# A pre-norm attention and expert layer on one core: where the attended values are transposed and divided

## The chip, the cores and the metric

One core of one Trainium2 chip. The metric is the device time of one execution, in microseconds (us). The kernel is written engine by engine: TensorE (PE) multiplies, VectorE (DVE), ScalarE (ACT) and GpSimd (POOL) work on elements, and SyncE (SP) issues every DMA. Each engine takes its instructions in program order, and they are tied together by semaphores.

## What is computed

The input is x, 32 sequences of 256 tokens of 128 features. Two residual layers follow each other. The first is attention with 16 heads of 8 features and a window of 128 tokens, the second a mixture of 16 experts of width 64 (4 chosen for each token, from 2 of 4 groups) beside one shared expert.

```python
x = x + attention(layernorm(x))        # softmax over keys j with i-128 <= j <= i, then @ w_out.T + b_out
x = x + experts(layernorm(x))          # sigmoid router, top 4 of 16, silu(g) * u, shared expert
def attention(x):
    q, k, v = split(x @ w_in.T + b_in)               # 16 heads of 8
    scores = where(allowed, q @ k.T / sqrt(8), -1e9)
    return (softmax(scores) @ v) @ w_out.T + b_out
```

All inputs and outputs are float32.

## The kernel before

The 8192 tokens are worked in 16 steps of 512 tokens (two sequences, called halves 0 and 1 below). All 16 steps of attention come first, then all 16 steps of experts; the rows after attention (x1) wait in device memory between the two.

**Attention.** The function `body(i)` of each engine holds one period of a software pipeline: the scores, exponentials and attended values of step i-1 ("now") and the projections and row maxima of step i ("prep"). Before the exponentials of a step the kernel needs the maximum of each row of scores. So TensorE first computes the scores once for their maxima (`score_maxima`, units 0 to 7 of a step, four per half; each unit fills two banks of PSUM, `ps_max`), VectorE reduces each bank to chunk maxima (`chunk_maxima`, line 910, two instructions per unit), and after four units `row_maxima` (lines 929 to 939) makes the row maxima, which SyncE writes to memory and loads back into the operands of the second computation (`load_max`). A unit may start only when both banks of the unit before it are reduced, since there is one pair of banks. The second computation is `scores` (units 0 to 9, five per half), whose two banks ScalarE turns into probabilities (`exps`, line 699); unit u+1 of `scores` waits for the exponentials of unit u, since there is again one pair of banks. `attend` and `attend_tails` multiply the probabilities with the values; the values carry a column of ones, so the sum of each row comes out beside them, in `ps_att`, transposed: features on partitions, tokens along the row.

**From attended values to x1, before.** ScalarE copies `ps_att` to SBUF (`take_att`, line 708); TensorE transposes it into `ps_b` (`transpose_att`, line 1434, four transposes per half); VectorE takes the reciprocal of the row sums and multiplies (`normalise`, lines 947 and 950); TensorE transposes the quotient into `ps_c` (`transpose_attn`, line 1448, two per half); ScalarE copies that (`take_attn`, line 716); TensorE multiplies with the output weights (`project_att`, line 1458); and VectorE adds the residual (`add_residual`, line 962).

**What else a period holds.** VectorE makes the statistics of the layer norm of the next step (`statistics(prep + 1)`, lines 867 and 874), spreads the queries (`spread_q`, line 888, four instructions) and makes the low parts of queries and keys (`low_part`, line 898). GpSimd normalises the next step (lines 521 to 536) and adds a constant vector to x for the residual (`residual`, line 552). When that sum is done, SyncE loads the next x into the same buffer (`load_x`, line 412), and `statistics` waits for that load. TensorE projects queries, keys (`project_qk`, line 1284) and values (`project_v`, line 1291) and transposes the normalised x (`transpose_x`, line 1270). ScalarE spreads the values (`spread_v`, line 687).

**What sets the order.** Nothing is scheduled by a tool: the order on each engine is that of the calls in its `body`, `last` (the last attention step, which also prepares the expert weights) and the loop over `d` for the experts.

**Experts.** Each step d has nine rounds. In each, TensorE computes gate and up projections of two experts (`up`, lines 1603 to 1605), ScalarE applies silu (line 799), VectorE multiplies (`gate`, line 1140), GpSimd multiplies by the routing weights (`weigh`, line 634), and TensorE multiplies down (`down`, line 1614). The routing of step d+2 is computed between the rounds. The 16 weights of each token are made by GpSimd (`scale_weight`, line 624), transposed by TensorE (`transpose_weights`, line 1591), copied by ScalarE (line 791), stored to memory and loaded back broadcast over 64 partitions (`store_weight`, `load_spread`).

The order of TensorE in a period of attention:

```python
scores(now, 5); attend(now, 0, 1); score_maxima(prep, 2); attend_tails(now, 0)
scores(now, 6); transpose_att(now, 0); score_maxima(prep, 3)
scores(now, 7); transpose_attn(now, 0); attend(now, 1, 0)
scores(now, 8); score_maxima(prep, 4); transpose_x(prep + 1); project_att(now, 0)
scores(now, 9); score_maxima(prep, 5); attend(now, 1, 1); attend_tails(now, 1); score_maxima(prep, 6)
```

## Time and profile before

| | us |
|---|---|
| median of 3 runs | 753.68 (753.0 to 758.73) |
| the profiled execution | 755.73 |
| its span, first to last instruction | 754.0 |
| TensorE busy in the span | 707.3 (94%) |
| VectorE busy | 580.1 (77%) |
| ScalarE busy | 364.2 (48%) |
| GpSimd busy | 299.5 (40%) |

The profile is one execution. Its rows give for each instruction the engine, the line of the kernel, the operation, output and input tiles, the start from the span's beginning and the duration. In a timeline several instructions of a line stand merged in one row, and the duration is then that of all; the ends of matmuls are modelled and overlap the next row, so what a piece of TensorE's work occupies is read from one start to the next. The attention steps fill the span from about 16 to 390 us, the experts from 394 us to the end.

### The profile page before, as it was taken

To read this page: it belongs to the slowest core of one execution; us is meant where nothing else is said; L and a number is where in the kernel's file an instruction comes from. 1 tells how busy PE (TensorE), PEld (TensorE's weight loads), DVE (VectorE), ACT (ScalarE), POOL (GpSimd) and SP (SyncE) were. 2 spreads that over 40 slices of the span, in tenths; PEclk is the share of its full clock that TensorE was granted. 3 is DMA by queue.
4 is the path that set the end of the run, shared out by engine and by line. 5 is a ranking of instruction groups with operands and counts; after the bars stand their busy time and mean duration, and the time that the engine had idled before them with its cause. 6 is when DMAs were issued, how large, how long until landed. Compare 5 with 4: busy or idle time off the path is not lost.

```text
span 754.0 us, 21748 instructions
## 1 busy us (share of the span) xinstructions
PE 707.3 (94%) x8499; PEld 472.1 (63%) x8499; DVE 580.1 (77%) x1745; ACT 364.2 (48%) x740; POOL 299.5 (40%) x320
## 2 busy tenths in 40 slices
PE   5697999899999999999778999999999999999997
PEld 3364666666666666666455666666666666666664
DVE  6676878788888888888477878887877888777632
ACT  3365666667677667666562332332333233233321
POOL 5212112122221122212205665666656666664543
PEclk9599999999999999999889999999999999999999
DMA  2244222233323232333118356664445666544560
GB/s 85 61 135 129 63 96 67 83 102 103 101 80 100 84 90 67 95 102 102 59 48 206 76 126 154 155 151 103 120 122 130 154 156 142 112 105 106 118 140 28
DMA packets 64885, 80.23 MB, mean 106 GB/s; under 512 B 10976, under 2 KB 38896, under 8 KB 64752
## 3 DMA queue, kind: packets, MB, share of 16 engines
q1 hardware_dynamic: 64784, 78.84, 40.0%
q8 instruction: 68, 1.11, 0.6%
q14 instruction: 33, 0.27, 0.1%
HBM read 61.00 MB, written 17.56 MB: 104 GB/s over the span
## 4 chain that ended last, share of the span: by engine, by line
PE 78%; DVE 8%; DMA 6%; ACT 4%; issue 2%; SPq 2%; POOL 1%; DVEq 0%; ACTq 0%; PEldq 0%; POOLq 0%
PE ps_c L1614 14%; PE ps_att L1399 7%; PE ps_sc L1373 6%; PE ps_max L1603 4%; PE ps_max L1329 4%; PE ps_max L1605 4%; PE ps_max L1604 4%; PE ps_sc L1347 4%; PE ps_sc L1604 4%; PE ps_sc L1605 4%; PE ps_sc L1603 4%; PE ps_a L1291 3%; ACT probs L699 3%; DMA xin<-in_L_attn_x_dram 2%; DVE chunkmax L910 2%; PE ps_c L1617 2%
## 5 line engine op out<-in xcount | busy, mean ns | idle before, releaser
L634 POOL TENSOR_TENSOR probs<-probs,stacks 128x512 f32<-128x512 f32 x128 | 165.1, 1290 | 125.8 <-DVE probs L1140 74.1
L799 ACT ACTIVATE probs<-ps_max 128x512 f32<-128x512 f32 x144 | 86.1, 598 | 220.2 <-PE ps_max L1605 216.6
L910 DVE TENSOR_REDUCE chunkmax<-ps_max 128x14 f32<-128x448 f32 (+1 forms) x250 | 151.7, 648 | 36.4 <-PE ps_max L1306 36.3
L699 ACT ACTIVATE probs<-ps_sc 128x512 f32<-128x512 f32 x256 | 138.9, 595 | 50.6 <-PE ps_sc L1347 49.6
L1140 DVE TENSOR_TENSOR probs<-probs,ps_sc 128x512 f32<-128x512 f32 x128 | 87.2, 682 | 69.5 <-PE ps_sc L1605 26.3
L1614 PE MATMUL ps_c<-probs,wd 128*128 128x512 f32 x256 | 130.3, 592 | 1.3 <-POOL probs L634 1.3
L1603 PE MATMUL ps_max<-xh,whigh 128*128 128x512 f32 x144 | 93.4, 649 | 2.9 <-DVE probs L1140 2.1
L552 POOL TENSOR_TENSOR xres<-xin,cvec 128x512 f32<-128x512 f32 x16 | 20.5, 1282 | 141.5 <-DVE x L962 141.1
L1373 PE MATMUL ps_sc<-stacks 32*64 32x192 f16 (+2 forms) x2048 | 64.4, 232 | 11.4 <-ACT probs L699 2.6
L1399 PE MATMUL ps_att<-probs,stacks 128*32 128x192 f32 (+1 forms) x1536 | 71.0, 319 | 0.0
L1373 PEld LDWEIGHTS ps_sc<-stacks 32*64 32x64 f16 x2048 | 36.6, 105 | 44.1 <-ACT probs L699 26.5
L521 POOL TENSOR_TENSOR veps<-meanvar,eps 128x4 f32<-128x4 f32 x32 | 6.4, 201 | 140.8 <-DVE meanvar L874 140.8
L1604 PE MATMUL ps_max<-xl,whigh 128*128 128x512 f32 x144 | 57.0, 396 | 0.0
L1605 PE MATMUL ps_max<-xh,wlow 128*128 128x512 f32 x144 | 56.9, 395 | 0.0
L1614 PEld LDWEIGHTS ps_c<-probs,wd 128*128 128x128 f32 x256 | 48.2, 189 | 13.5 <-POOL probs L634 1.7
L1329 PE MATMUL ps_max<-hl,qdiag 32*128 32x160 f16 x1000 | 48.6, 216 | 8.0 <-DVE chunkmax L910 7.1
L1399 PEld LDWEIGHTS ps_att<-probs,stacks 128*32 128x32 f32 x1536 | 44.2, 112 | 16.8 <-issue 3.1
L1604 PE MATMUL ps_sc<-xl,whigh 128*128 128x512 f32 x128 | 50.8, 397 | 0.0
L1605 PE MATMUL ps_sc<-xh,wlow 128*128 128x512 f32 x128 | 50.8, 397 | 0.0
L1603 PE MATMUL ps_sc<-xh,whigh 128*128 128x512 f32 x128 | 50.5, 394 | 0.0
L1347 PE MATMUL ps_sc<-edges,repeat 64*128 64x192 bf16 (+2 forms) x576 | 49.9, 243 | 0.0
L1329 PEld LDWEIGHTS ps_max<-hl,qdiag 32*128 32x128 f16 x1000 | 31.2, 93 | 26.6 <-DVE chunkmax L910 15.0
(167 smaller groups left out, 1253.7 us busy)
## 6 DMA issues: line engine op xcount, KB each, us to landing
stacks<-weight_scratch SPq DMA_DIRECT2D x32, 1024.0 KB, 9.9
stacks<-qk_scratch SPq DMA_DIRECT2D x48, 256.0 KB, 3.2
qk_scratch<-hl SPq DMA_DIRECT2D x32, 256.0 KB, 3.5
xin<-in_L_attn_x_dram SPq DMA_DIRECT2D x16, 256.0 KB, 3.5
x_scratch<-x SPq DMA_DIRECT2D x16, 256.0 KB, 2.2
xin<-x_scratch SPq DMA_DIRECT2D x16, 256.0 KB, 9.1
xres<-x_scratch SPq DMA_DIRECT2D x16, 256.0 KB, 9.3
out_dram<-result SPq DMA_DIRECT2D x16, 256.0 KB, 9.2
```

What stands on the lines that cost most here:

```text
L634: nc.gpsimd.tensor_tensor(inter[p % 3], gated[p % 2], spread[d % 2][:, p, :], ALU.mult).then_inc(inter_ready, 1)
L699: nc.scalar.activation(dst[:, :], ps_sc[s][:, 0:dst.shape[1]], ACT.Exp, scale=SCALE).then_inc(probs_ready, 1)
L799: nc.scalar.activation(silu[n % 2][rows, :], ps_max[n % 2][rows, :], ACT.Silu).then_inc(silu_ready, 1)
L910: nc.vector.tensor_reduce(chunkmax[:, 2 * pair + m, at:at + CHUNKS[h]], max_banks(d, u)[m][:, 0:BANK_COLS[h]].rearrange("p (n k) -> p n k" ...
L1140: tt(gated[p % 2], silu[n % 2], ps_sc[n % 2][:, :], ALU.mult).then_inc(gated_ready, 1)
L1329: mm(banks[m][:, at:at + width], qdiag[rows, b * NB + n, :, :].rearrange("p c k -> p (c k)"), hl[rows, 0, 1, b * S + key0:b * S + key0 + w ...
L1373: mm(dst, qkstack[p][rows, 1, jj, q0:q0 + TB], qkstack[p][rows, 0, jj, q0:q0 + QCOLS[m]].rearrange("p (n k) -> p n k", k=TB), start=(at == ...
L1399: last = mm(ps_att[32 * x:32 * x + 32, half * S + TB * m:half * S + TB * m + QCOLS[m]].rearrange("p (n k) -> p n k", k=TB), vdiag[p][:, (b ...
L1603: mm(bank[slot][:, :], whigh[:, q, :], xh[d % 3][:, :], start=True, stop=False)
L1604: mm(bank[slot][:, :], whigh[:, q, :], xl[d % 3][:, :], start=False, stop=False)
L1605: last = mm(bank[slot][:, :], wlow[:, q, :], xh[d % 3][:, :], start=False, stop=True)
L1614: last = mm(ps_c[:, :], wd[:, p, :], inter[p % 3], start=(p == 0), stop=False)
```

## The change

**Attended values.** ScalarE's two copies and TensorE's six transposes per half are gone. VectorE transposes `ps_att` by blocks of 32x32 into `att_rows` (`take_att`, one instruction of 128x512), divides there (`normalise`, which writes the features in another order), and transposes the quotient again by blocks of 32x32 into `attTn` (128x256). The output weights are put into the same order once at the start, for which ScalarE makes one copy more and TensorE one transpose more, and one more copy and transpose serve the constant vector.

**Chunk maxima.** The two banks of a unit are one tensor now, reduced by one instruction.

**Orders.** TensorE's order in `body` is another (below), and ScalarE spreads the values after unit 6 of the exponentials instead of after unit 4. GpSimd's `residual` also waits for `spread_q` of its step.

**Routing weights.** VectorE transposes them by blocks of 32x32 (`transpose_weights`, 128x64, after round 1 of a step), SyncE stores them with four DMAs instead of one, and TensorE's four transposes and ScalarE's copy per step are gone.

```diff
@@ SyncE, store_weight
-                sp.wait_ge(weightT_ready, d + 1)
+                sp.wait_ge(weightQ_ready, d + 1)
                 after(sp, spread_loaded[d % 2], 32 * (d // 2))
-                sp.dma_start(wt_d[d % 2], weightT[d % 2][:, :]).then_inc(weight_stored[d % 2], 16)
+                dst = wt_d[d % 2].rearrange("n t -> (n t)").rearrange("(b q i k) -> i q b k", b=2, q=32, i=4, k=32)
+                for i in range(4):
+                    sp.dma_start(dst[i], weightQ[d % 2][32 * i:32 * i + 32, :].rearrange("q (b k) -> q b k", b=2)
+                                 ).then_inc(weight_stored[d % 2], 16)
@@ GpSimd, residual
                 after(pool, x1_ready, 2 * d - 2)
+                pool.wait_ge(qdiag_ready, d + 1)
                 pool.wait_ge(x_loaded[d % 2], 16 * (d // 2 + 1))
@@ ScalarE, body
                 exps(now, 4)
+                exps(now, 5)
+                exps(now, 6)
...
                 spread_v(prep)
-                exps(now, 5)
-                take_att(now, 0)
-                exps(now, 6)
                 exps(now, 7)
-                take_attn(now, 0)
@@ VectorE
-                for m in range(2):
-                    dve.wait_ge(max_full, 16 * d + 2 * u + m + 1)
-                    nc.vector.tensor_reduce(chunkmax[:, 2 * pair + m, at:at + CHUNKS[h]],
...
+                dve.wait_ge(max_full, 8 * d + u + 1)
+                nc.vector.tensor_reduce(chunkmax[:, 2 * pair:2 * pair + 2, at:at + CHUNKS[h]],
+                                        max_banks(d, u)[:, :, 0:BANK_COLS[h]].rearrange("p m (n k) -> p m n k", k=KB),
+                                        AX.X, ALU.max).then_inc(max_free, 1)
...
+            def take_att(d, b):
...
+                dve.wait_ge(pv_done, 6 * d + 3 * b + 3)
+                after(dve, att_ready, 2 * d + b)
+                nc.vector.transpose(att_rows[:, :], ps_att[:, :]).then_inc(att_rows_ready, 1)
...
-                view = ps_b[:, :].rearrange("p (n k) -> p n k", k=16)
-                dve.wait_ge(att_tr_done, 2 * d + b + 1)
+                view = att_rows[:, :].rearrange("p (n k) -> p n k", k=16)
+                dve.wait_ge(att_rows_ready, 2 * d + b + 1)
                 nc.vector.reciprocal(rden[:, :], view[:, :, HD]).then_inc(nd_chain, 1)
                 dve.wait_ge(nd_chain, 2 * d + b + 1)
...
+                nc.vector.tensor_tensor(att[:, :].rearrange("p (n h d) -> p h n d", h=2, d=HD),
+                                        att_rows[:, :].rearrange("p (h n k) -> p h n k", h=2, k=16)[:, :, :, 0:HD],
+                                        rden[:, :].rearrange("p (h n) -> p h n", h=2).unsqueeze(3).to_broadcast([P, 2, 16, HD]),
+                                        ALU.mult).then_inc(att_ready, 1)
+                dve.wait_ge(att_ready, 2 * d + b + 1)
+                after(dve, proj_done, 2 * d + b)
+                nc.vector.transpose(attTn[:, :], att[:, :]).then_inc(attTn_ready, 1)
@@ VectorE, body
                 chunk_maxima(prep, 2)
+                take_att(now, 0)
                 normalise(now, 0)
...
                 add_residual(now, 0)
+                take_att(now, 1)
                 chunk_maxima(prep, 6)
...
@@ TensorE, body
                 scores(now, 0)
-                transpose_att(now - 1, 1)
                 project_v(prep, 0)
                 score_maxima(now, 7)
+                project_v(prep, 3)
                 scores(now, 1)
-                transpose_attn(now - 1, 1)
...
                 score_maxima(prep, 2)
+                scores(now, 6)
                 attend_tails(now, 0)
-                scores(now, 6)
-                transpose_att(now, 0)
+                project_v(prep, 2)
                 score_maxima(prep, 3)
                 scores(now, 7)
-                transpose_attn(now, 0)
                 attend(now, 1, 0)
+                score_maxima(prep, 4)
                 scores(now, 8)
-                score_maxima(prep, 4)
                 transpose_x(prep + 1)
```

TensorE, from the attended values of half 1 (`attend(now, 1, 0)`) to the transposes of x, before. `ps_sc` with `stacks` are the scores (unit 8), `ps_max` with `hl` the maxima (unit 4):

```order
L1399 MATMUL ps_att<-probs,stacks 32x192 x8
L1399 MATMUL ps_att<-probs,stacks 32x128 x4
L1373 MATMUL ps_sc<-stacks 64x3x64 x8
L1373 MATMUL ps_sc<-stacks 64x2x64 x4
L1347 MATMUL ps_sc<-edges,repeat 128x192 x2
L1347 MATMUL ps_sc<-edges,repeat 128x128 x2
L1329 MATMUL ps_max<-hl,qdiag 128x160 x6
L1329 MATMUL ps_max<-hl,qdiag 128x32 x2
L1306 MATMUL ps_max<-edges,repeat 128x3x2x32 x2
L1306 MATMUL ps_max<-edges,repeat 128x32 x2
L1270 MATMUL ps_a<-ident,xhat 128x128 x4
```

The same place in the changed program (line numbers are its own):

```order
L1396 MATMUL ps_att<-probs,stacks 32x192 x8
L1396 MATMUL ps_att<-probs,stacks 32x128 x4
L1327 MATMUL ps_max<-hl,qdiag 128x160 x6
L1327 MATMUL ps_max<-hl,qdiag 128x32 x2
L1304 MATMUL ps_max<-edges,repeat 128x3x2x32 x2
L1304 MATMUL ps_max<-edges,repeat 128x32 x2
L1370 MATMUL ps_sc<-stacks 64x3x64 x8
L1370 MATMUL ps_sc<-stacks 64x2x64 x4
L1344 MATMUL ps_sc<-edges,repeat 128x192 x2
L1344 MATMUL ps_sc<-edges,repeat 128x128 x2
L1268 MATMUL ps_a<-ident,xhat 128x128 x4
```

The maxima of unit 4, which wait for VectorE's reduction of unit 3, stood behind the scores of unit 8 and now stand ahead of them.

VectorE, from the statistics to the row maxima, before:

```order
L867 BN_STATS stats<-xin 128x6 x4
L874 BN_AGGR meanvar<-stats 128x2 x4
L910 TENSOR_REDUCE chunkmax<-ps_max 128x16 x2
L947 RECIPROCAL rden<-ps_b 128x32
L950 TENSOR_TENSOR att<-ps_b,rden 128x256
L910 TENSOR_REDUCE chunkmax<-ps_max 128x14 x2
L929 TENSOR_REDUCE rowmax<-chunkmax 128x4x3
```

The same place in the changed program:

```order
L839 BN_STATS stats<-xin 128x6 x4
L846 BN_AGGR meanvar<-stats 128x2 x4
L881 TENSOR_REDUCE chunkmax<-ps_max 128x2x16
L918 STREAM_TRANSPOSE att_rows<-ps_att 128x512
L926 RECIPROCAL rden<-att_rows 128x32
L929 TENSOR_TENSOR att<-att_rows,rden 128x2x16x8
L935 STREAM_TRANSPOSE attTn<-att 128x256
L881 TENSOR_REDUCE chunkmax<-ps_max 128x2x14
L900 TENSOR_REDUCE rowmax<-chunkmax 128x4x3
```

Between the chunk maxima of units 2 and 3 two instructions (lines 947 and 950) have become four, and each pair of reductions is one of twice the columns.

## Rows read from the trace of the kernel before

**Rows 1.** Busy us by stretch: PE, PEld, DVE, ACT, POOL; then clock, DMA share, GB/s.
```profile
200.00:300.00 100.00, 97.91 (x2074) 65.88 (x2072) 85.42 (x249) 69.26 (x146) 22.82 (x25) 1.00 0.27 86
...
500.00:600.00 100.00, 100.00 (x403) 66.85 (x401) 82.86 (x261) 32.47 (x62) 61.28 (x58) 1.00 0.59 140
```

**Rows 2.** Timeline, TensorE (start us, us, line, tiles).
```profile
201.37 0.66 PE L1434 MATMUL ps_b<-ident,attT 128*128 128x128 f32 x4
201.96 0.37 PE L1329 MATMUL ps_max<-hl,qdiag 32*128 32x160 f16 x8
...
202.49 0.41 PE L1373 MATMUL ps_sc<-stacks 32*64 32x192 f16 x12
...
203.08 0.44 PE L1448 MATMUL ps_c<-ident,att 128*128 128x128 f32 x2
203.45 1.08 PE L1399 MATMUL ps_att<-probs,stacks 128*32 128x192 f32 x24
204.45 0.41 PE L1373 MATMUL ps_sc<-stacks 32*64 32x192 f16 x12
...
206.51 0.32 PE L1373 MATMUL ps_sc<-stacks 32*64 32x64 f16 x16
...
208.68 0.40 PE L1329 MATMUL ps_max<-hl,qdiag 32*128 32x160 f16 x8
...
222.74 0.66 PE L1434 MATMUL ps_b<-ident,attT 128*128 128x128 f32 x4
```

**Rows 3.** Timeline, VectorE, same stretch.
```profile
203.97 0.58 DVE L929 TENSOR_REDUCE rowmax<-chunkmax 128x12 f32<-128x60 f32 x6
...
204.80 0.21 DVE L939 STREAM_TRANSPOSE rowmaxT<-rowmax 128x32 f16<-128x32 f16 x1
...
214.04 2.07 DVE L888 TENSOR_SCALAR qdiag<-hl,headrow 128x512 f16<-128x512 f16 x4 [0.24 <-ACT hl L672]
...
220.27 0.86 DVE L867 BATCH_NORM_STATS2 stats<-xin 128x6 f32<-128x128 f32 x4
...
221.60 1.26 DVE L910 TENSOR_REDUCE chunkmax<-ps_max 128x16 f32<-128x512 f32 x2
```

**Rows 4.** Timeline, GpSimd: the residual sum and the centring.
```profile
201.99 1.04 POOL L526 TENSOR_TENSOR xcent<-xin,meanvar 128x512 f32<-128x512 f32 x1
...
213.88 1.29 POOL L552 TENSOR_TENSOR xres<-xin,cvec 128x512 f32<-128x512 f32 x1 [9.72 <-DVE x L962]
```

**Rows 5.** Line 888, VectorE, whole span (ns min/median/max).
```profile
L888 DVE TENSOR_SCALAR qdiag<-hl,headrow x64: 334/341/1282, 14.4 to 342.5; 128x512 f16<-128x512 f16 x64
```

**Rows 6.** VectorE groups by form, 100 to 340 us.
```profile
L910 DVE TENSOR_REDUCE chunkmax<-ps_max 128x16 f32<-128x512 f32 x90 | 57.4, 679 | 9.5 <-PE ps_max L1306 9.5
L910 DVE TENSOR_REDUCE chunkmax<-ps_max 128x14 f32<-128x448 f32 x92 | 52.9, 616 | 13.8 <-PE ps_max L1306 13.8
...
L950 DVE TENSOR_TENSOR att<-ps_b,rden 128x256 f32<-128x256 f32 x23 | 9.8, 424 | 0.8
...
L947 DVE RECIPROCAL rden<-ps_b 128x32 f32<-128x32 f32 x23 | 8.1, 352 | 4.3 <-PE ps_b L1434 4.3
...
L939 DVE STREAM_TRANSPOSE rowmaxT<-rowmax 128x32 f16<-128x32 f16 x23 | 4.9, 211 | 0.8
```

**Rows 7.** Line 412, the loads of x, 100 to 340 us.
```profile
DMA to landing us min/median/max: 3.0/3.6/4.5
```

**Rows 8.** VectorE groups by form, 430 to 700 us.
```profile
L1122 DVE TENSOR_TENSOR chosen<-picked,score 128x64 f32<-128x64 f32 x12 | 15.2, 1269 | 0.4
...
L1119 DVE TENSOR_TENSOR picked<-replaced,ps_a 128x64 f32<-128x64 f32 x12 | 2.6, 213 | 0.0
```

**Rows 9.** Timeline, TensorE, experts.
```profile
581.26 0.60 PE L1591 MATMUL ps_b<-ident,weight 128*16 128x128 f32 x4
581.62 0.48 PE L1603 MATMUL ps_max<-xh,whigh 128*128 128x512 f32 x1
```

**Rows 10.** Timeline, GpSimd, between the two phases.
```profile
403.02 1.26 POOL L634 TENSOR_TENSOR probs<-probs,stacks 128x512 f32<-128x512 f32 x1 [5.37 <-DMA stacks<-weight_scratch]
```

More of the change, by code:

```diff
@@ L170, in build_block @@
         share = sb("share", [P, NT], FP32)
[L171 to L172 removed]
+        weight = sb("weight", [P, NE, NT], FP32)
+        weightQ = [sb(f"weightQ{p}", [P, NE * NT], FP32) for p in range(2)]
         silu = [probs[n][:, :] for n in (0, 1)]
@@ L1132, in shares, with transpose_weights @@
                 nc.vector.reciprocal(share[:, :], total1[:, :]).then_inc(share_ready, 1)
+            def transpose_weights(d):
+                if not valid(d):
+                    return
+                dve.wait_ge(weight_ready, d + 1)
+                after(dve, weight_stored[d % 2], 64 * (d // 2))
+                nc.vector.transpose(weightQ[d % 2][:, :], weight[:, :, :].rearrange("p n t -> p (n t)")
+                                    ).then_inc(weightQ_ready, 1)
             def gate(d, p):
@@ L1176, in last @@
                 split_weight(3)
+                take_att(now, 0)
                 normalise(now, 0)
@@ L1193, in last @@
                 invert(1)
+                take_att(now, 1)
                 normalise(now, 1)
@@ L1338, in score_maxima @@
                         g = 2 * pair + m
-                        last = masks(banks, m, [window], slice(32 * g, 32 * g + 32), (32 * g, 0))
-                        if w == len(windows) - 1:
-                            last.then_inc(max_full, 1)
+                        last = masks([banks[:, n, :] for n in range(2)], m, [window], slice(32 * g, 32 * g + 32), (32 * g, 0))
+                last.then_inc(max_full, 1)
             def mask2(s, cols, edge):
@@ L1463, in _ @@
             pe.wait_ge(w_loaded, 16 * 2)
-            for n in range(4):
-                last = nc.tensor.transpose(ps_b[:, n * P:(n + 1) * P], wraw[:, n, :], ident[:, :])
-            last.then_inc(wt_done, 1)
+            for n in range(3):
+                nc.tensor.transpose(ps_b[:, n * P:(n + 1) * P], wraw[:, n, :], ident[:, :])
+            pe.wait_ge(wo_turned, 1)
+            nc.tensor.transpose(ps_b[:, 3 * P:4 * P], wo_order[:, :], ident[:, :]).then_inc(wt_done, 1)
+            nc.tensor.transpose(ps_sc[0][:, 0:E], wraw[:, 3, :], ident[:, :]).then_inc(wo_done, 1)
             pe.wait_ge(b_loaded, 16 * 2)
@@ L1530, in transpose_weight @@
                         last = nc.tensor.transpose(bank[:, t * P:(t + 1) * P], xhat[:, t, :], ident[:, :])
-                elif what[0] == "weight":
-                    pe.wait_ge(weight_ready, 1)
-                    for t in range(NT):
-                        last = nc.tensor.transpose(bank[0:NE, t * P:(t + 1) * P], weight[:, t, :], ident[:, :])
-                    last.then_inc(weight_tr_done, 1)
-                    pe.wait_ge(weight_tr_done, 1)
-                    pe.sem_inc(fw_done, 1)
-                    return
                 elif what[0] == "sh":
@@ L1582, in route @@
                 last.then_inc(logit_done, 1)
-            def transpose_weights(d):
-                if not valid(d):
-                    return
-                pe.wait_ge(weight_ready, d + 1)
-                after(pe, result_ready, d - 2)
-                for t in range(NT):
-                    last = nc.tensor.transpose(ps_b[0:NE, t * P:(t + 1) * P], weight[:, t, :], ident[:, :])
-                last.then_inc(weight_tr_done, 1)
             def up(d, p):
```

159 lines of the change are left out of this document (50 added, 109 removed).

## The prediction

> **What bounds the kernel now.** I read the busy time by stretch first. In attention TensorE is busy in 97.9 of 100 us at the full clock and VectorE in 85.4; among the experts TensorE is busy in all of 100 us and VectorE in 82.9 [rows 1]. So TensorE sets the pace of both phases, but in attention VectorE stands only 15% behind it. Then the timeline of TensorE. The same transpose of half 0 comes at 201.37 and at 222.74 [rows 2], so a period of attention lasts 21.37 us, and there are 15 of them between the first body and the last step. In that timeline scores follow scores: unit 7 starts at 202.49 and unit 8 at 204.45 [rows 2]. Unit 8 needs the exponentials of unit 7, and 1.96 us is what that round through ScalarE costs; whatever TensorE does inside it is free. From unit 9 at 206.51 to the maxima of unit 6 at 208.68 [rows 2] lie 2.17 us of work in one piece. The timeline of VectorE then shows what its part of a period is made of [rows 3, 6].
>
> **What leaves TensorE.** Per half, four transposes from 201.37 to 201.96 and two from 203.08 to 203.45 [rows 2]: 0.59 + 0.37 = 0.96 us, so 1.9 us per period. If TensorE stayed the bound, a period would be 21.37 - 1.9 = 19.5 us; since some of these transposes lie inside a 1.96 us round, 20.0 is nearer. That is the first rival. ScalarE loses copies that nobody is short of.
>
> **What VectorE gains and loses.** (a) The first transposition, 128x512 float32 out of PSUM. The trace has only one such operation, 128x32 in float16, at 211 ns [rows 6]. For the slope I use the reductions: 679 against 616 ns for 64 columns more [rows 6], 0.98 ns a column. 211 + 480 x 0.98 = 0.68 us, and the reduction of 512 columns says the same. I take 0.7. Below, it will hardly beat that reduction, so 0.68; above, float32 may cost two passes, 211 + 2 x 480 x 0.98 = 1.15 us. (b) The second, 128x256 in SBUF: 211 + 224 x 0.98 = 0.43 us, with 0.42 (the product of that shape [rows 6]) and 0.65 as ends. (c) Two reductions of 679 become one of 679 + 512 x 0.98 = 1.18, and two of 616 one of 616 + 448 x 0.98 = 1.06. Before, such a pair took 1.26 us [rows 3], since the second starts before the first is quite done, so a unit wins 0.08 at most, 0.6 per period. (d) The four spreading instructions take 2.07 us together [rows 3], though the median of one is 0.34 and the longest 1.28 [rows 5]: the first of them waits out GpSimd's residual sum, which runs from 213.88 to 215.17 [rows 4]. With the new wait GpSimd comes after them, and 0.94 us per period is won. (e) The multiplication (0.42 [rows 6]) read PSUM and SBUF and now reads SBUF twice. Among the experts the product of two SBUF tiles takes 1.27 us while its neighbour of the same shape with one operand in PSUM takes 0.21 [rows 8]; it waits out a GpSimd instruction. In attention GpSimd's centring of 1.04 us [rows 4] and what follows it lie just behind the statistics, where the division of half 0 now comes.
>
> In sum VectorE has per period 2 x (0.7 + 0.43) = 2.3 us more and 1.5 less. It was busy for 0.854 x 21.37 = 18.3 us and will be for about 19.1. That is too near 20 to be hidden by itself, so the order of waits decides.
>
> The Trainium skill (SBUF — State Buffer, Who interferes with whom) says that a VectorE instruction with two SBUF inputs and a GpSimd instruction that reads SBUF fully block each other, the later one waiting for the earlier. Rows 8 agree. By that rule (e) costs between nothing and one GpSimd instruction at half 0; the sum below carries 0.3 for it, from the rows.
>
> The Trainium skill (Vector Engine (DVE) Microarchitecture Reference, The reshape front-end and per-opcode configuration) says that a transposing instruction sustains one element per cycle and lane, and makes no exception for four-byte elements. No row here shows a float32 one. By that rule the two-pass price of (a) falls away; I keep it as a rival, since only a run can tell.
>
> **The loop that closes.** In the new order each thing waits for the one before, all around a period. I start where `attend_tails` of half 1 is done.
> 1. VectorE: transposition 0.75 with its hand-over; maxima 6, 1.13; division of half 1 (reciprocal 0.36, product 0.42, transposition 0.43, links) 1.23; maxima 7, 1.00; row maxima 1.04, from 203.97 to 204.80 + 0.21 [rows 3]; residual add, of the product's shape, 0.35; spreading 2.07 - 0.94 = 1.13. Together 6.6.
> 2. Only now GpSimd: residual sum 1.29 [rows 4]; only then SyncE loads the next x, which lands after 3.6 us (3.0 to 4.5) [rows 7]; hand-overs 0.2. Together 5.1. Beside it the low parts and maxima 0 and 1 of VectorE are done in about 4.5, so VectorE waits some 0.6 for x.
> 3. VectorE: statistics from 220.27 to 221.60, 1.33 [rows 3]; maxima 2, 1.13; transposition 0.75; division of half 0, 1.23, with 0.3 for GpSimd. Together 4.7.
> 4. Maxima 3, 1.06 and 0.06 to TensorE. TensorE: maxima 4, 0.5 (as from 201.96 to 202.49 [rows 2]), which now stand ahead of scores 8; the round from scores 8 to scores 9, 1.96; from scores 9 to the end of the tails 2.17 and 0.1. Together 5.9.
>
> Sum 22.3 us. Before, the loop was open at step 4 (scores 8 stood ahead of maxima 4, so a late reduction of unit 3 did not delay them) and in step 2 (GpSimd started beside the spreading). I take 22.1 for the period, 0.7 over the old one: the landing is as often below as above 3.6, and not each link will be the last in each period. TensorE, 1.9 us lighter, then waits some 2.5 us in each period for VectorE. Over 15 periods: +10.5 us (21.5 to 22.8: +2 to +21).
>
> **The rest.** Among the experts four transposes go from 581.26 to 581.62 [rows 9], 0.36 us, with the change of kind around them up to 0.6, in 15 steps: -6 us (-5 to -9). VectorE does 128x64 instead, 0.25 us, behind round 1, where it has 15% of idle time; four stores instead of one take SyncE some 1 us more, but start earlier. Between the phases GpSimd waits 5.4 us for the first weights at 403.02 [rows 10]; they leave TensorE's queue, where they stood behind eight other transposes, so -1 (-2 to +1). The start has two copies and two transposes more: +0.5 (0 to 1).
>
> Sum: 10.5 - 6 - 1 + 0.5 = +4. The profiled execution took 755.73 us, so its like would take 759.7; the median of the runs shown is 753.68, 2 us lower, and the forecast against it is 757.7, with a range of its own of 750 to 768.
>
> **Rivals.** What differs by 1%, 7.5 us, can be told from no change.
> - TensorE stays the bound: the load of x lands early, the reductions keep ahead, and a period is 20.0 us. 15 x 1.4 = 21 and 6 and 1 less: 726 us. For it speaks VectorE's busy sum of 19.1, below 20; against it, that steps 1 to 4 are serial by the semaphores and VectorE would have no idle time at all, though it now waits for TensorE before most reductions [rows 6]. Chance 0.13. Between it and the forecast (21.4 or less, 747 or under) another 0.05.
> - The forecast: 0.62. About a quarter of it lies above 1%.
> - Two passes for float32: 0.45 us more for each first and 0.22 for each second transposition, all four in the loop: 22.1 + 1.3 = 23.4, so 757.7 + 15 x 1.3 = 777 us. It decides from about 0.9 us per 128x512. Against it, the float16 row pays hardly anything over other small operations. Chance 0.08.
> - The product of half 0, and the spreading, run into GpSimd again: where maxima 2 come 0.3 later than I put them, the product finds not the end of the centring but the whole next instruction, 1.04 instead of 0.3, and GpSimd's output comes later to TensorE too. 15 x 0.8 = 12: 770 us. Chance 0.12.
>
> Faster by over 1% then has 0.13 + 0.05 = 0.18, slower 0.08 + 0.12 + 0.16 = 0.36, and 0.46 lies within. The range leaves out the first rival and the dearest: 746 to 773.
>
> **What would show it.** Right: a period of 21.8 to 22.4 between two equal rows of TensorE; TensorE waiting about 1.2 us for line 881 before the maxima of unit 4 in each period, and below 92% busy from 100 to 340 us; the statistics of VectorE waiting for the load of x in most periods, which they do in hardly any now; spreading instructions all near 0.34; the 128x512 transposition at 0.7. Wrong: VectorE idle before its reductions as before with TensorE still at 98%, which would be the first rival; a transposition of over 0.9 us; products of over 1 us in the division. Among the experts TensorE stays at 100% and a step is 0.4 us shorter.

## The result, and the profile after

| | before | after |
|---|---|---|
| median of the runs | 755.51 us (753.0 to 758.73) | 765.67 us (763.82 to 770.84) |
| the profiled execution | 755.73 | 770.84 |
| its span | 754.0 | 769.0 |
| mean granted clock of TensorE in it | 0.974 | 0.946 |
| TensorE, VectorE, ScalarE busy | 707.3, 580.1, 364.2 | 693.9, 593.0, 330.0 |

The changed kernel takes 1.0143 times the time of before (95% interval 1.0074 to 1.0213), some 10 us more. The profiled execution, 770.84, is the longest of its four runs; a second profile of the same kernel (below) has a span of 762.4 us at a clock of 0.959. Runs more than 1.5% above the fastest of the same kernel are left out of all medians and ratios.

The busy time by stretch, after (columns as in [rows 1]; 100:200 is new beside them):

```profile
100.00:200.00 100.00, 89.22 (x1893) 58.83 (x1892) 82.70 (x214) 57.63 (x119) 19.69 (x21) 0.96 0.25 78
200.00:300.00 100.00, 85.34 (x1912) 56.80 (x1912) 81.14 (x207) 57.33 (x120) 22.05 (x25) 0.98 0.29 92
...
500.00:600.00 100.00, 100.00 (x392) 66.50 (x391) 82.22 (x262) 31.54 (x62) 62.64 (x61) 1.00 0.54 128
```

TensorE fell from 97.9 to 85.3 us of 100 in attention and is still at 100 among the experts. VectorE has more work in all, but not a greater share of each 100 us (81 to 83 against 85.4): neither engine is full, so what grew is waiting. The clock column matters later: before it is 1.00 from 100 to 300 us, and here it is 0.96 and 0.98.

One piece of VectorE's and of TensorE's timeline, after. This is the stretch that steps 3 and 4 of the forecast describe:

```profile
205.66 0.87 DVE L839 BATCH_NORM_STATS2 stats<-xin 128x6 f32<-128x128 f32 x4 [1.71 <-DMA xin<-in_L_attn_x_dram]
...
207.00 1.19 DVE L881 TENSOR_REDUCE chunkmax<-ps_max 128x32 f32<-128x1024 f32 x1
208.11 0.71 DVE L918 STREAM_TRANSPOSE att_rows<-ps_att 128x512 f32<-128x512 f32 x1
...
209.24 0.52 DVE L929 TENSOR_TENSOR att<-att_rows,rden 128x256 f32<-128x256 f32 x1
209.79 0.45 DVE L935 STREAM_TRANSPOSE attTn<-att 128x256 f32<-128x256 f32 x1
210.16 1.05 DVE L881 TENSOR_REDUCE chunkmax<-ps_max 128x28 f32<-128x896 f32 x1
```

```profile
208.25 0.37 PE L1327 MATMUL ps_max<-hl,qdiag 32*128 32x160 f16 x8 [1.47 <-DVE chunkmax L881]
...
208.65 0.41 PE L1370 MATMUL ps_sc<-stacks 32*64 32x192 f16 x12
...
211.27 0.40 PE L1327 MATMUL ps_max<-hl,qdiag 32*128 32x160 f16 x8 [0.96 <-DVE chunkmax L881]
...
211.70 0.41 PE L1370 MATMUL ps_sc<-stacks 32*64 32x192 f16 x12
```

The statistics wait 1.71 us for the load of x. Everything behind them is late by it: the reduction of unit 2 releases TensorE's maxima 3 at 208.25 after 1.47 us of idle time, the reduction of unit 3, behind the four instructions of the division, releases maxima 4 at 211.27 after 0.96. Scores 7 (208.65) and scores 8 (211.70) are 3.05 us apart, where [rows 2] had 1.96. In a period of after in which no load is late they are still 2.86 apart (230.36 and 233.22).

The waits between 100 and 340 us, eleven periods (us in total, times, longest):

```profile
DVE chunkmax L881 <- PE ps_max L1304: 22.2, 28, 2.9
...
PE ps_max L1327 <- DVE chunkmax L881: 16.0, 20, 1.7
...
DVE stats L839 <- DMA xin<-in_L_attn_x_dram: 4.6, 3, 1.9
```

Before, over the same stretch:

```profile
PE ps_max L1329 <- DVE chunkmax L910: 0.2, 1, 0.2
```

VectorE waited for TensorE's maxima before too (23.3 us, 46 times). What is new is the other direction, 16.0 us in which TensorE waits for the reductions. And one period on the chain of waits of after:

```profile
267.87 1.14 POOL xres L557
269.01 5.36 DMA xin<-in_L_attn_x_dram
...
278.98 0.99 DVE chunkmax L881
...
280.01 0.40 PE ps_max L1327 x8
```

In this period the chain passes through the steps of the forecast one by one, with a load of x that took 5.4 us where I had 3.6. The row above it misleads, as an experiment showed: GpSimd's residual sum is not what held this load back.

**Where the 15 us of the two profiled executions lie.** The first and the last of the spreadings of the queries mark 15 periods, TensorE's first gate projection marks the experts. After:

```profile
L860 DVE TENSOR_SCALAR qdiag<-hl,headrow x64: 342/348/355, 14.4 to 359.3; 128x512 f16<-128x512 f16 x64
```

```profile
L1555 PE MATMUL ps_max<-xh,whigh x144: 395/794/798, 414.0 to 759.4; 128*128 128x512 f32 x144
```

The same row of before for the projections ([rows 5] has the spreadings, 14.4 to 342.5):

```profile
L1603 PE MATMUL ps_max<-xh,whigh x144: 466/762/798, 394.2 to 744.4; 128*128 128x512 f32 x144
```

| us | start | 15 periods | between the phases | experts | at 1.2 GHz, 30 to 350 us |
|---|---|---|---|---|---|
| before | 14.4 | 328.1 | 51.7 | 359.8 | 13 |
| after | 14.4 | 344.9 | 54.7 | 355.0 | 40 |
| after, again | 14.9 | 337.6 | 53.6 | 356.3 | 22 |

The last column is summed from the granted clock in stretches of 4 us: a stretch at 0.57 is mostly at 1.2 GHz, one at 1.00 wholly at 2.4 GHz. Up to 350 us, all of it lies ahead of 100 us in before; in after 16 us lie behind. Between the phases every kernel here has some: from 352 to 464 us before has 14 us and after 30.

### The profile page after: what moved, and what is told of

It reads as the page before. It is cut to its first block, busy times and chain, and to the rows that moved or that the text cites. A ratio compares the mean times of both kernels' runs of the same rounds, so it can differ in the third digit from the quotient of the medians.

```text
span 769.0 us, 21082 instructions
## 1 busy us (share of the span) xinstructions
PE 693.9 (90%) x8244; PEld 458.8 (60%) x8244; DVE 593.0 (77%) x1697; ACT 330.0 (43%) x662; POOL 301.5 (39%) x320
## 4 chain that ended last, share of the span: by engine, by line
PE 64%; DVE 18%; issue 6%; DMA 6%; ACT 3%; SPq 1%; POOL 1%; DVEq 0%; ACTq 0%
PE ps_c L1566 14%; DVE chunkmax L881 5%; PE ps_max L1555 5%; PE ps_max L1557 4%; PE ps_max L1556 4%; PE ps_att L1396 4%; DMA xin<-in_L_attn_x_dram 4%; PE ps_sc L1370 4%; PE ps_sc L1556 4%; PE ps_sc L1555 4%; PE ps_sc L1557 4%; PE ps_max L1327 3%; PE ps_sc L1344 3%; DVE att_rows L918 2%; PE ps_c L1569 2%
## 5 line engine op out<-in xcount | busy, mean ns | idle before, releaser
L881 DVE TENSOR_REDUCE chunkmax<-ps_max 128x28 f32<-128x896 f32 (+1 forms) x125 | 142.2, 1138 | 35.6 <-PE ps_max L1304 35.3
L1370 PE MATMUL ps_sc<-stacks 32*64 32x192 f16 (+2 forms) x2048 | 67.0, 240 | 17.1 <-ACT tails L704 6.9
L1327 PE MATMUL ps_max<-hl,qdiag 32*128 32x160 f16 x1000 | 50.2, 221 | 34.2 <-DVE chunkmax L881 27.7
L1396 PE MATMUL ps_att<-probs,stacks 128*32 128x192 f32 (+1 forms) x1536 | 76.1, 336 | 0.0
L1370 PEld LDWEIGHTS ps_sc<-stacks 32*64 32x64 f16 x2048 | 38.2, 109 | 50.2 <-issue 20.9
L1396 PEld LDWEIGHTS ps_att<-probs,stacks 128*32 128x32 f32 x1536 | 46.1, 116 | 18.2 <-issue 0.7
L1555 PEld LDWEIGHTS ps_max<-xh,whigh 128*128 128x128 f32 x144 | 27.5, 191 | 39.1 <-issue 37.0
```

What stands on the lines that cost most here:

```text
L881: nc.vector.tensor_reduce(chunkmax[:, 2 * pair:2 * pair + 2, at:at + CHUNKS[h]], max_banks(d, u)[:, :, 0:BANK_COLS[h]].rearrange("p m (n k ...
L1327: mm(banks[:, m, at:at + width], qdiag[rows, b * NB + n, :, :].rearrange("p c k -> p (c k)"), hl[rows, 0, 1, b * S + key0:b * S + key0 + w ...
L1370: mm(dst, qkstack[p][rows, 1, jj, q0:q0 + TB], qkstack[p][rows, 0, jj, q0:q0 + QCOLS[m]].rearrange("p (n k) -> p n k", k=TB), start=(at == ...
L1396: last = mm(ps_att[32 * x:32 * x + 32, half * S + TB * m:half * S + TB * m + QCOLS[m]].rearrange("p (n k) -> p n k", k=TB), vdiag[p][:, (b ...
L1555: mm(bank[slot][:, :], whigh[:, q, :], xh[d % 3][:, :], start=True, stop=False)
```

## The experiments

Ratios are to the kernel before, run beside each group of experiments (medians 755.55 us for the first four, 756.58 for the next four, 755.72 for the last four), with 95% intervals. They are not made from the two medians, and times of different groups are compared only to 1 us or so.

**The changed kernel once more,** unedited, as the ground for the next ones.

> The changed kernel once more, as the one to compare the others of this call with. Expected as measured: 1.010 to 1.018 of the kernel before, TensorE waiting 1.0 us or more for line 881 ahead of the maxima of unit 4, and the statistics waiting for the load of x in some periods.

Measured: 762.80 us, 1.0100 (1.0064 to 1.0136). Together with the first result the loss is 1.0 to 1.4%. In what follows after is 762.8.

**The load of x first.** SyncE takes its work in order too, and in its body the next x stood behind the loading back of the row maxima and the store of x1.

```diff
@@ SyncE, body
+                load_x(i + 1)
                 load_max(i - 1, 1)
                 store_x1(i - 2)
-                load_x(i + 1)
```

> Only SyncE's order changes: load_x of a period is issued ahead of the second load_max and the store of x1, which it does not depend on. Theory A (the landing of x, issued behind the round trip of the row maxima, is in the loop that closes a period): the statistics wait for no load, a period is about 0.4 us shorter and the long ones of over 23 us are gone, 6 to 10 us less than the changed kernel. Rival B (the loop is closed by VectorE and TensorE alone, the load is beside it): no change, within 2 us.

Measured: 753.22 us, 0.9976 (0.995 to 1.0002): 9.6 us less than after, from this one move. The queue of SyncE and GpSimd's residual sum, after:

```profile
221.04 0.33 SPq L400 DMA_DIRECT2D max_scratch<-rowmaxT  x1
...
222.46 0.55 SPq L402 DMA_DIRECT2D stacks<-max_scratch  x1
222.47 1.27 POOL L557 TENSOR_TENSOR xres<-xin,cvec 128x512 f32<-128x512 f32 x1 [11.81 <-issue]
...
223.54 0.43 SPq L413 DMA_DIRECT2D xin<-in_L_attn_x_dram  x1
```

and with the load first:

```profile
207.71 0.44 SPq L413 DMA_DIRECT2D xin<-in_L_attn_x_dram  x1
...
215.80 1.26 POOL L557 TENSOR_TENSOR xres<-xin,cvec 128x512 f32<-128x512 f32 x1 [11.82 <-issue]
...
220.33 0.86 DVE L839 BATCH_NORM_STATS2 stats<-xin 128x6 f32<-128x128 f32 x4
```

In after the load starts at 223.54, while this period's residual sum still runs (until 223.74): it doesn't wait for that sum but for the one before, long done, and was held only by its place behind the store (221.04) and the loading back (222.46) of the row maxima and the store of x1. Moved ahead it starts 8 us before the residual sum, and the statistics wait for nothing. Its 15 periods are 334.1 us (337.6 without) and the stretch between the phases 49.6 (53.6): the same queue also carries the x1 that the experts' first statistics need. So of the 9 us between these two executions 3.5 lie in the periods and 4.0 between the phases. The forecast for the period itself was missed: its commonest length stays 21.52 us, and three periods of over 23 us are left (26.5, 23.4 and 24.6), all three with a clock below 1.00. The late load is not what makes the period long where the clock is full.

**Maxima 4 behind scores 8,** as before, alone and with the load first.

```diff
@@ TensorE, body
                 attend(now, 1, 0)
-                score_maxima(prep, 4)
                 scores(now, 8)
+                score_maxima(prep, 4)
```

> Only TensorE's order changes: the maxima of unit 4 stand behind the scores of unit 8 again, as before the change. Theory A: the late reduction of unit 3 no longer holds up scores 8, and a period is 0.65 us shorter, 10 us less than the changed kernel. Rival C (VectorE's greater work alone makes the period, whatever TensorE's order): within 2 us of the changed kernel. Rival D (the changed order of TensorE was needed for something else): slower by 3 us or more.

Measured: 759.17 us, 1.0071 (1.0041 to 1.01), 3.6 us less than after.

> The edits of e1 and e2 together. Theory A: a period of about 21.2 us, 0.95 less than the changed kernel's, so 13 to 16 us less than it, and as fast as the kernel before or up to 5 us faster, since the experts' part is 5 us shorter. If only one of the two closes the loop, the better one of e1 and e2 and no more.

Measured: 753.08 us, 0.9979 (0.9956 to 1.0001), nothing on top of the load, though the commonest period is 21.31 to 21.40 us and not 21.52. TensorE's wait for the reductions did go, and came back as a wait for ScalarE. With the load first alone, then with both, 100 to 340 us:

```profile
PE ps_max L1327 <- DVE chunkmax L881: 12.9, 19, 0.8
...
PE ps_sc L1370 <- ACT probs L704: 2.0, 10, 0.2
```

```profile
PE ps_sc L1370 <- ACT probs L704: 9.1, 11, 0.8
...
PE ps_max L1327 <- DVE chunkmax L881: 3.9, 7, 0.6
```

**Without GpSimd's new wait.**

```diff
@@ GpSimd, residual
-                pool.wait_ge(qdiag_ready, d + 1)
```

> The changed kernel without GpSimd's wait for the spreading of the queries. The prediction's step 2 put the residual sum, which that wait delays, into the loop. Theory A1 (as that step has it): x is loaded earlier, 2 to 9 us less than the changed kernel. Theory A2 (the load of a period needs only the residual sum of the period before; it is SyncE's queue that holds it): no gain from it, and one spreading instruction of about 1.27 us per period again, so the same time within 3 us.

Measured: 766.94 us, 1.0126 (1.0067 to 1.0185), no gain; that it is slower than after (1.0100) is not shown. The statistics still waited for x (7.6 us in 6 times between 30 and 370 us, against 9.2 in 6), and taking away the wait of the residual sum hardly brought x earlier: the second reading that the load isn't held by that sum. What came back is the collision of [rows 3, 5], in VectorE's groups:

```profile
L859 DVE TENSOR_SCALAR qdiag<-hl,headrow 128x512 f16<-128x512 f16 x60 | 31.5, 586 | 2.4 <-ACT hl L676 2.3
```

Its mean was 347 ns with the wait. So the wait does what the forecast said for VectorE, 0.95 us per period.

**Filling TensorE's idle time.** Both edits above, and six transposes of the identity per period into a part of `ps_c` that nothing reads there (work of no use), four ahead of scores 8 and two ahead of maxima 3.

```diff
@@ TensorE, body
+                for _ in range(4 if valid(now) else 0):
+                    nc.tensor.transpose(ps_c[:, 0:P], ident[:, :], ident[:, :])
                 scores(now, 8)
```

> e3_both with six TensorE transposes more per period, of the identity into columns of ps_c that nothing reads there, put ahead of scores 8 (four) and of the maxima of unit 3 (two), where TensorE waits. Theory E (in attention the idle TensorE is granted the lower clock now and then, and each such stretch makes a period 2 to 3 us longer): no stretch at the lower clock after 100 us, and 2 to 5 us less than e3_both. Rival F (those long periods have another cause, and 0.7 us of work more per period costs what it takes): the same or up to 8 us more.

Measured: 753.0 us, 0.9943 (0.9902 to 0.9985), against 753.08 without them. TensorE is busier (92.15 us of 200 to 300), the time at 1.2 GHz is 18 us (19.7 without), and stretches of it remain at 162 to 174 and 210 to 218 us. This settles nothing about their cause: 0.7 us of work a period may have been too little or in the wrong place. One run of this kernel took 744.98 us at a mean clock of 0.981, where the other six that count have 0.963 to 0.967: how much time goes at 1.2 GHz differs between runs of one program.

**The routing weights alone,** on the kernel before: VectorE's 128x64 transposition and the four stores in place of TensorE's four transposes and ScalarE's copy.

```diff
@@ TensorE, experts
-                    if p == 2:
-                        transpose_weights(d + 1)
@@ VectorE, experts
                 gate(d, 1)
+                transpose_weights(d + 1)
```

> The kernel before with the change of the routing weights alone: VectorE transposes them, four stores, no TensorE transposes, the first weights no longer in TensorE's queue. Attention as before. Forecast of the prediction for this part: 6 us less among the experts and 1 between the phases, so 0.990 to 0.994 of the kernel before. Rival: VectorE's 0.25 us per step and the four stores give it back, 0.998 to 1.002.

Measured: 750.74 us, 0.9902 (0.9866 to 0.9938). The experts take 356.1 us against 359.8; the stretch between the phases is unchanged (51.6 against 51.7).

**The changed kernel without its title.** The weights, the merged reductions, GpSimd's wait and the load first, on the kernel before: attended values, TensorE's and ScalarE's order are the old ones.

> All parts that leave the attended values on their old path: the routing weights of e6, one reduction per unit, GpSimd's wait for the spreading, and SyncE's load of x first. TensorE's order is that of before. If the loss sits in the attended values on VectorE and TensorE's order alone, this is the fastest of all: e6 and 2 to 5 us less from a lighter VectorE (0.94 us of waiting and 0.5 of reduction less per period, of which TensorE, the bound, sees 0.1 to 0.3), 0.985 to 0.991 of the kernel before. If one of the other parts costs time, it is slower than e6.

Measured: 741.03 us, 0.9774 (0.9705 to 0.9843): 12 us less than the changed kernel with the load first, and the fastest of all, more than was expected. Its period is 20.99 or 21.00 us in all but one behind the third. TensorE, 200 to 300 us:

```profile
200.00:300.00 100.00, 98.01 (x2098) 66.39 (x2100) 80.13 (x209) 69.99 (x149) 19.52 (x21) 1.00 0.29 89
```

**Which of them gave that.** Two parts of it by themselves:

```diff
@@ one reduction per unit, and GpSimd's wait: VectorE, GpSimd
-                for m in range(2):
-                    dve.wait_ge(max_full, 16 * d + 2 * u + m + 1)
+                dve.wait_ge(max_full, 8 * d + u + 1)
...
+                pool.wait_ge(qdiag_ready, d + 1)
```

> The kernel before with two edits of the change only: one reduction per unit in place of two, and GpSimd's residual sum waiting for the spreading of the queries. SyncE's order, the routing weights, the attended values and TensorE's order are those of before. It splits the 9.7 us that lie between the kernel before with the weights' edit alone (750.7 us) and that kernel with merged reductions, wait and early load of x (741.0). Theory R (VectorE's lighter work gave them): 745 to 748 us here against some 755.5, and the run with weights and early load stays at 750. Theory L (the load of x gave them, as it gave 9.6 us in the changed kernel): 754 to 757 here, and 741 to 744 there.

Measured: 751.22 us, 0.9934 (0.9898 to 0.997). The other part is the kernel before with the weights' edit and the load of x first.

> The kernel before with the routing weights' edit and the early load of x, nothing else. Theory L: 741 to 744 us. Theory R: 749 to 752 us. If both this and the run with reductions and wait gain about half, the gains add and neither alone is the cause.

Measured: 745.28 us, 0.9848 (0.981 to 0.9886). Neither theory alone: reductions and wait give 4.5 us, the load some 5 beyond the weights' 6, and 4.5 + 10.4 is the 15 us of the kernel with all. Between the phases the load gains 4.6 us in the old order (47.0 against 51.6 with the weights alone). The 15 periods of the two profiled executions are 5.6 us apart as well (321.5 and 327.1), with 4 us less at 1.2 GHz, but this one is the fastest of its five runs by 3 us, and how much of the 5.6 is the load's was not tested.

**The attended values alone.** The changed kernel with the load first, and with the order of before on TensorE and ScalarE, less the transposes and copies. It differs from the 741 us kernel only in where the attended values are transposed and divided.

```diff
@@ TensorE, body
-                project_v(prep, 3)
                 scores(now, 1)
...
-                project_v(prep, 1)
+                project_v(prep, 3)
                 project_qk(prep, 1)
                 scores(now, 3)
+                project_v(prep, 1)
...
                 scores(now, 4)
+                project_v(prep, 2)
...
-                scores(now, 6)
                 attend_tails(now, 0)
-                project_v(prep, 2)
+                scores(now, 6)
...
-                score_maxima(prep, 4)
                 scores(now, 8)
+                score_maxima(prep, 4)
```

> The changed kernel with the load of x first (753.2 us), and with TensorE's and ScalarE's order of the kernel before, less the transposes and copies that the change took out. It differs from the 741.0 us kernel only in where the attended values are transposed and divided. Theory V (VectorE's longer row closes the loop whatever the order): 750 to 756 us, period 21.5, TensorE waiting for the reductions in both orders. Theory O (the attended values on VectorE are harmless, TensorE's new order cost the 12 us): 735 to 742 us, period 20.5 to 21.

Measured: 751.54 us, 0.9939 (0.9903 to 0.9974). The moved values cost 10.5 us in the old order as well (12.5 by the two ratios). But the period that was expected with it, 21.5 us, is wrong. TensorE is busy in 36.58 of the 40 us from 260 to 300, at the full clock. Its scores where the removed transposes stood (6, 7, 8, then 0, 1, 2):

```profile
288.79 0.41 PE L1370 MATMUL ps_sc<-stacks 32*64 32x192 f16 x12
...
290.68 0.41 PE L1370 MATMUL ps_sc<-stacks 32*64 32x192 f16 x12 [0.27 <-ACT probs L704]
...
292.57 0.41 PE L1370 MATMUL ps_sc<-stacks 32*64 32x192 f16 x12 [0.23 <-ACT probs L704]
...
297.62 0.41 PE L1370 MATMUL ps_sc<-stacks 32*64 32x192 f16 x12 [0.32 <-issue]
...
299.51 0.41 PE L1370 MATMUL ps_sc<-stacks 32*64 32x192 f16 x12 [0.19 <-ACT probs L704]
...
301.59 0.41 PE L1370 MATMUL ps_sc<-stacks 32*64 32x192 f16 x12
```

At the full clock a period here is 21.05 us, just that of before. TensorE has 1.9 us less to do and doesn't get round sooner. The chain of waits shows most of the reason; one round of this kernel on it:

```profile
290.68 0.41 PE ps_sc L1370 x12
291.09 0.29 PE ps_sc L1344 x4
...
291.43 1.09 ACT probs L704 x2
```

Scores, masks, exponentials and their hand-overs fill the 1.89 us from 290.68 to 292.57, and no other work of TensorE's that leaves this round can shorten it. The timeline of before at the same places, in a period of 21.05 us:

```profile
243.04 0.41 PE L1373 MATMUL ps_sc<-stacks 32*64 32x192 f16 x12
...
244.93 0.41 PE L1373 MATMUL ps_sc<-stacks 32*64 32x192 f16 x12
...
246.90 0.41 PE L1373 MATMUL ps_sc<-stacks 32*64 32x192 f16 x12
...
251.56 0.41 PE L1373 MATMUL ps_sc<-stacks 32*64 32x192 f16 x12
...
253.45 0.41 PE L1373 MATMUL ps_sc<-stacks 32*64 32x192 f16 x12
...
255.93 0.41 PE L1373 MATMUL ps_sc<-stacks 32*64 32x192 f16 x12
```

Scores 6 to 7, 7 to 8, 0 to 1 and 1 to 2 took 1.89, 1.97, 1.89 and 2.48 us, 8.23 together, and take 1.89, 1.89, 1.89 and 2.08, 7.75. Of 1.9 us of transposes 0.5 stood outside a round that ScalarE sets; the rest had filled TensorE's wait for the exponentials. The 0.5 came back too: from scores 9 to scores 0 it is 3.00 us now (294.62 to 297.62) and was 2.61. Ahead of scores 0 TensorE is idle for 0.32 us; of the loads that scores 0 needs by the semaphores the row maxima's is the last to be issued (295.71), and VectorE's longer row makes them, but the trace names no releaser there. TensorE also still waits for the reductions (8.4 us in 20 times from 100 to 340 us; 0.2 in before).

So where the clock is full and no wait is added, the moved values cost nothing against before (21.05 in both) and 0.06 us a period against the 741 us kernel (20.99), 1 us of the 10.5. The rest goes mostly with the time at 1.2 GHz: 39 us between 30 and 350 us, 13 in the 741 us kernel. The first projection of the queries, two matmuls of 512 columns, takes 0.97 us from start to start at the full clock (300.09 to 301.06) and 1.86 at 1.2 GHz (234.50 to 236.36), so 26 us more at the lower clock cost up to 13, and the 15 periods are 11.8 us longer (332.9 against 321.1). What brings the lower clock about is not shown by this.

**The first transposition twice,** on the changed kernel with the load first; the first result is not used.

```diff
+                nc.vector.transpose(att_again[:, :], ps_att[:, :])
                 nc.vector.transpose(att_rows[:, :], ps_att[:, :]).then_inc(att_rows_ready, 1)
```

> The changed kernel with the load of x first (753.2 us), and VectorE making the 128x512 transposition of the attended values twice, the first time into a tile that nothing reads: 2 x 0.70 us more of VectorE per period and nothing else. It measures what a microsecond of VectorE is worth here. If VectorE's chain is the closed loop in all places: 15 periods x 1.4 = 21 us more, 774. If only the transposition of one half stands in the loop that closes: 764. If VectorE's work is hidden beside TensorE: 753 to 756. TensorE's busy share should fall in step with the first two, and with it more time at the lower clock.

Measured: 788.82 us, 1.0411 (1.0363 to 1.0458), 36 us more where the dearest theory had 21. The profiled executions differ by 33.4 us (spans 786.9 and 753.5). The time at 1.2 GHz is 59 us, 32 more than in the kernel it is made from, worth up to 16: 21 and up to 16 hold the 33. The two periods wholly at the full clock behind the third are 23.2 us, 1.7 more than the 21.52 of the kernel it is made from. Nearly each of the others has a stretch at the lower clock; the one at 146 us, behind a gap of TensorE:

```profile
144.00:146.00 2.00, 0.26 (x10) 0.04 (x4) 1.93 (x4) 0.77 (x2) 0.17 (x1) 1.00 0.00 0
146.00:150.00 4.00, 4.00 (x58) 2.93 (x60) 2.02 (x9) 1.12 (x3) 0.00 (x0) 0.57 0.03 4
```

## Why the time came out near the forecast, and what in its mechanism did not hold

The forecast was +4 us on the execution, 757.7 against the runs shown; measured are +10.2 and +7.3. It gave 0.36 to a loss of over 1% and 0.46 to a change within 1%, and the loss is 1.0 to 1.4%. Direction and range came out. The waits at steps 3 and 4 are there; that one loop through all four steps sets the period is not what the runs show, and the nearness of the number is in part luck. Term by term, against the two profiled executions:

| us | forecast | measured |
|---|---|---|
| 15 periods | +10.5 | +16.8, +9.5 |
| between the phases | -1 | +3.0, +1.9 |
| experts | -6 | -4.8, -3.5 |
| start | +0.5 | 0, +0.5 |

**What leaves TensorE.** 1.9 us per period is right as a count and was never to be had: 0.5 of it stood outside the rounds with ScalarE, and in the old order even that came back as a wait. Step "20.0 is nearer" failed, and the first rival with it; the round of 1.96 us stood in the prediction, but I didn't lay the four transposes against it one by one. [Rows 2] has each of them between two scores.

**VectorE's prices.** In the groups by form, 100 to 340 us, after (the second transposition has a mean of 445 ns there):

```profile
L918 DVE STREAM_TRANSPOSE att_rows<-ps_att 128x512 f32<-128x512 f32 x21 | 14.8, 706 | 0.9 <-PE ps_att L1414 0.9
```

0.706 against 0.7 and 0.445 against 0.43, so the one-pass price was right and the third rival falls. Merged reductions took 1.20 and 1.07 in the mean (forecast 1.18 and 1.06), the spreading 0.348 each and never 1.28. The product took 0.438 in the mean, 0.637 at most: the fourth rival, a division that waits out GpSimd, didn't come. In the timeline above the product of half 0 took 0.52, 0.1 over the plain one.

**The loop.** Steps 3 and 4 are there as written: maxima 4 waiting for the reduction of unit 3 behind the division, and scores 8 behind them, 2.86 to 3.05 us after scores 7. Undoing the order of step 4 alone gave 3.6 us back. Step 2 is not in the loop that sets the common period: with the load first, when no statistics wait for x, that period is 21.52 us all the same. It only makes single periods longer, and it named the wrong holder. That "only then SyncE loads the next x", behind this period's residual sum, is not what the semaphores say: the load needs the sum of the period before. The load waits in SyncE's queue behind the row maxima's way through memory. They come from VectorE too, so the load was often about as late as forecast; but the remedy that step 2 suggests, an earlier residual sum, gained nothing, and the move of one line of SyncE's gained 9.6 us, more than half of it outside the 15 periods. The statistics waited for x in 6 of the 15 periods in one profile of after and in 8 in the other, where the forecast said most.

**The size of the period.** I took 21.37 us for before from one pair of rows. From the starts of GpSimd's residual sum seven of the eleven periods behind the fourth are 21.04 or 21.05. After, the shortest are 21.52, 0.47 more and not 0.7; the others of the eleven are 21.8 to 25.5, where the forecast put one number for all. They are longer where the statistics waited for x (two of its loads took over 5 us, not 3.6) and where TensorE ran at 1.2 GHz. The second had no term at all. Of the +16.8 and +9.5 us only 15 x 0.47 = 7 is the longer common period; the rest lies in single periods. That the second of them stands so near the +10.5 of the forecast is luck: a common period overrated by 0.2 us, and no term for the long ones. TensorE's share of 85 to 89% (forecast: below 92) was not only the sign of the wait; it came with a lower clock, which no row of before from 100 to 350 us shows.

**Between the phases,** -1 was argued from GpSimd's first wait for weights [rows 10]. It did shrink, from 5.37 to 4.05 us, but it lies behind the first projection, in the experts' part. What grew before it was the last step's attention, with more time at 1.2 GHz, and the wait of the statistics for x1 (3.75 us, 2.92 before): with that load first the stretch is 49.6.

**Experts.** A step took 22.03 us before and takes 21.77 in the mean of twelve, between two equal instructions of VectorE behind 430 us. The transposes are thus worth 0.26 us a step, 4 us in all (4.8 and 3.5 in the two profiles, 3.7 on the kernel before), and not the 0.4 that -6 stood for. Their own 0.36 us [rows 9] didn't come back whole, though TensorE stayed at 100%, and the change of kind around them added nothing. Where the missing 0.1 us is stays open.

**Why the change is slower,** then: it takes from TensorE work that mostly filled waits, gives VectorE 2.3 us a period that stand in its in-order row ahead of reductions TensorE waits for, delays thereby the load of x through SyncE's queue, and leaves TensorE gaps that go with half a clock. Its other parts gain about 10 us (5.8 and 4.5), so the moved values, the new order and the late load together cost 17.5 to 20.5. That the clock falls because of the gaps is the one link of this account that is not shown.

**What stays open.** That the stretches at 1.2 GHz come from the gaps of TensorE is only an association: from 100 to 350 us they came in all kernels whose share in attention is 84 to 93% and in none of those at 96 to 98%, and the one trial to fill the gaps changed nothing. Nor does a gap suffice: before has one of 1.45 us (below) without such a stretch. Another cause that goes with the moved values isn't ruled out. Whether the attended values on VectorE would be free at an unbroken clock was not tried. Nor are the two orders of TensorE told apart with the load first: 751.5 and 753.2 us overlap, a shorter period with more time at 1.2 GHz against a longer with less.

## What to carry to other kernels

Before work is taken off the busiest engine, lay each piece against the round in which it stands: inside a producer-consumer round that another engine sets, it is free, and taking it out only turns busy time into waiting. Where an engine's in-order row grows, follow what it releases through every queue, the DMA issuer's above all; a load that needs nothing new can stand behind a round trip through memory, and moving it costs one line. Judge the parts of a mixed change apart: here the weights, the reductions and GpSimd's wait gain 15 us with that one line, and the moved values hid it.

## What the runs showed of the hardware that was not expected

The granted clock falls in the middle of a running pipeline. In after:

```profile
237.00:239.00 2.00, 0.73 (x32) 0.46 (x21) 2.00 (x4) 0.00 (x0) 0.00 (x0) 1.00 0.03 8
239.00:241.00 2.00, 1.98 (x40) 1.41 (x44) 1.83 (x5) 1.09 (x2) 0.00 (x0) 1.00 0.04 8
241.00:245.00 4.00, 4.00 (x36) 2.27 (x38) 2.18 (x11) 1.77 (x3) 0.00 (x0) 0.57 0.02 2
```

TensorE was busy for 0.73 of 2 us, then worked again at the full clock, and only then ran at 1.2 GHz for most of 4 us, at 100% busy. Here the fall comes when the gap is over, and it hits work. Not every gap is followed by one: the 1.47 us at 208.25 above stands in a stretch without. Ahead of this gap the row maxima, stored at 233.88, could be loaded back only at 236.48, 2.6 us later, where 1.4 is usual. Such a wait is not new in after: before has it once, when 3.45 us lay between the same two DMAs, and there the clock stays at 1.00. After, then before:

```profile
239.02 0.41 PE L1370 MATMUL ps_sc<-stacks 32*64 32x192 f16 x12 [1.28 <-issue]
```

```profile
145.83 0.41 PE L1373 MATMUL ps_sc<-stacks 32*64 32x192 f16 x12 [1.45 <-issue]
```

The second finding is what a microsecond of VectorE costs in such a loop: 1.4 us more a period made 2.1 (365.2 us for the 15 periods against 334.1), where the two periods at the full clock show 1.7. The rest goes with more time at 1.2 GHz.
